# A four-layer model on one core: the second layer's channel mix changes stream, and score products go in pairs of 64-row tiles

## Time and profile before

| what | value |
| --- | --- |
| median of 3 runs | 1272.8 us (1272.34 to 1273.24) |
| the profiled execution, its own time | 1274.41 us |
| its span in the profile | 1272.4 us |
| mean granted TensorE clock | 0.936 of full |
| instructions | 14341 |

### The profile page before, as it was taken

How to read it: one execution, slowest core, us unless ns; L and a number is a source line. 1 busy time by engine, 2 the same in 40 slices (tenths; PEclk the granted TensorE clock), 3 DMA queues, 4 the chain that set the end, 5 groups by cost and what they waited for, 6 DMA issues and landing times.

```text
span 1272.4 us, 14341 instructions
## 1 busy us (share of the span) xinstructions
PE 1124.9 (88%) x5396; PEld 760.6 (60%) x5396; DVE 859.5 (68%) x1152; ACT 501.7 (39%) x1542; POOL 106.6 (8%) x92
## 2 busy tenths in 40 slices
PE   7867889997988999989898879899899998898888
PEld 4634656565755666657565565557656566477665
DVE  4599799688965798799745794466954569444320
ACT  1003125722582257325831624325533255232641
POOL 1020011001100100011000110001020010100000
PEclk8878889998999989989998999998999899899889
DMA  9100000000000000000000000000000000000000
GB/s 368 35 1 0 1 26 5 1 1 25 5 1 1 25 5 2 1 18 13 1 17 9 5 1 1 34 3 10 1 1 33 1 13 1 1 17 1 13 1 17
DMA packets 13895, 22.65 MB, mean 18 GB/s; under 512 B 3841, under 2 KB 10625, under 8 KB 13186
## 3 DMA queue, kind: packets, MB, share of 16 engines
q1 hardware_dynamic: 13826, 21.74, 5.1%
HBM read 16.48 MB, written 2.10 MB: 15 GB/s over the span
## 4 chain that ended last, share of the span: by engine, by line
PE 63%; DVE 24%; ACT 5%; issue 4%; POOL 3%; DMA 1%; SPq 0%; DVEq 0%; POOLq 0%; ACTq 0%
PE PA L1097 7%; PE QA L1003 6%; DVE S_ L509 5%; PE PB L1128 5%; PE QA L1315 5%; PE QB L990 4%; PE QB L1227 3%; PE PA L1036 3%; ACT big L923 3%; DVE az L378 3%; PE QA L1243 3%; DVE A L517 2%; PE QA L990 2%; DVE A L437 2%; PE QA L1306 2%
## 5 line engine op out<-in xcount | busy, mean ns | idle before, releaser
L923 ACT ACTIVATE big<-QB,nmax 128x128 f32<-128x128 f32 x512 | 181.4, 378 | 88.2 <-DVE nmax L632 88.1
L509 DVE TENSOR_TENSOR_SCAN S_<-W_,A 128x1024 f32<-128x1024 f32 x64 | 149.0, 2349 | 0.2
L1128 PE MATMUL PB<-A,common_w 128*128 128x256 f32 x512 | 131.3, 400 | 11.4 <-DVE A L517 11.4
L632 DVE TENSOR_REDUCE nmax<-QB 128x4 f32<-128x512 f32 x128 | 87.1, 685 | 65.6 <-PE QB L1227 41.4
L1128 PEld LDWEIGHTS PB<-A,common_w 128*128 128x128 f32 x512 | 98.3, 201 | 34.6 <-DVE A L517 15.1
L1097 PE MATMUL PA<-rwkv_w,X 128*128 128x256 f32 x384 | 100.8, 416 | 16.8 <-DVE X L416 16.6
L923 ACT ACTIVATION_READ_ACCUMULATOR big<-QB,nmax 128x1 f32 x512 | 111.8, 218 | 0.0
L1227 PE MATMUL QB<-big,QX 128*128 128x256 f32 x384 | 102.8, 392 | 0.0
L1097 PEld LDWEIGHTS PA<-rwkv_w,X 128*128 128x128 f32 x384 | 78.1, 209 | 34.3 <-DVE X L416 21.6
L1243 PE MATMUL QA<-common_w,big 128*128 128x128 f32 x512 | 83.8, 289 | 12.5 <-ACT XT L932 5.9
L1243 PEld LDWEIGHTS QA<-common_w,big 128*128 128x128 f32 x512 | 63.1, 147 | 40.5 <-issue 24.3
(11 more groups left out here) (160 smaller groups left out, 1871.5 us busy)
## 6 DMA issues: line engine op xcount, KB each, us to landing
rwkv_w<-in_rwkv_w SPq DMA_DIRECT2D x2, 2674.0 KB, 14.4
QX<-big SPq DMA_DIRECT2D x96, 32.0 KB, 1.9
attn_w<-in_attn_w SPq DMA_DIRECT2D x2, 1031.5 KB, 16.7
mlp_w<-in_mlp_w SPq DMA_DIRECT2D x1, 2052.0 KB, 23.5
X<-in_x SPq DMA_DIRECT2D x4, 512.0 KB, 13.1
ctx<-in_ctx SPq DMA_DIRECT2D x4, 512.0 KB, 4.2
ctx<-in_ctx_t SPq DMA_DIRECT2D x4, 512.0 KB, 3.5
out<-XT SPq DMA_DIRECT2D x8, 256.0 KB, 2.0
```

The source lines that it names most:

```text
L509: last = v.tensor_tensor_scan(S_[:, d].rearrange("p k t -> p (k t)"), W_[:].rearrange("p k t -> p (k t)"), A_[c % 2][:, d].rearrange("p k ...
L632: v.tensor_reduce(nmax[:, n % 2], bank(2 + n % 2).rearrange("p (j s) -> p j s", j=JH), AX.X, ALU.max, negate=True).then_inc(sem["a_max"], 1)
L923: last = s.activation(PR[:, n % 2, j], bank(2 + n % 2)[:, j * T:(j + 1) * T], ACT.Exp, bias=nmax[:, n % 2, j:j + 1], accum_out=den[:, b, h ...
L1128: last = t.matmul(y, ident, A_[c % 2][:, :, k], start=(c % 2 == 0 and k == 0), stop=False, skip_group_check=True)
```

## The change

It has two parts, with new `ORDER` strings of all engines.

**Channel mix.** It becomes a function of its own on each engine. For the first layer it stays in stream A with the same buffers. For the second layer it is the end of stream R (unit kind `mixer_ffn`): all its products go to PB, its buffers are parts of the recurrence's `A_` and `S_`, it has norm buffers of its own, and since Wk, Wr and Wv share PB, TensorE waits for Relu before `fWr` (g_kr) and for Tanh before `fWv` (g_rr). Three of the last unit's fills (16, 2 and 24 products) go away with it. The next unit's recurrence writes to `A_` after it.

**Scores.** `scores(m)` now issues a pair of jobs: two mask products with 64 rows each, in the tiles at rows 0 and 64, and four float32 products, alternating between the two tiles, one tile's into one bank of QB and the other's into the other bank. For the first sequence the tiles have 32 rows at 0 and 64, or 32 and 96. `QX` has three buffers in which two jobs share 128 rows, so its DMAs wait for no product any more. The pair waits for the exponentials of **both** jobs of the pair ahead. The number of products of each kind stays the same.

```
@@ scores
-                    def scores(n):
-                        b, i = divmod(n, QUAD)
+                    def scores(m):
+                        b, r = divmod(m, 2)
...
-                        if n >= 2:
-                            pe.wait_ge(sem["a_exp"], u.at("a_exp", n - 1))
-                        rows = slice(32 * i, 32 * i + 32)
-                        mask = mrow[:, b * T:(b + 1) * T].unsqueeze(1).broadcast_to([P, JH, T])
-                        t.matmul(bank(2 + n % 2), first_row[:], mask, start=True, stop=False, skip_group_check=True)
-                        if b and i == 0:
-                            pe.wait_ge(q_spread[b % 2], ...)
+                        else:
+                            pe.wait_ge(sem["a_exp"], u.at("a_exp", 2 * m))
+                        for g in range(2):
+                            half = slice(64 * g, 64 * g + 64)
+                            mask = mrow[half, b * T:(b + 1) * T].unsqueeze(1).broadcast_to([64, JH, T])
+                            t.matmul(bank(2 + g), first_row[half], mask, start=True, stop=False,
+                                     tile_position=(64 * g, 0), skip_group_check=True)
+                        if b and r == 0:
+                            pe.wait_ge(q_spread[b - 1], 16 * QUAD * (u.index + 1))
                         for h in range(HALF):
-                            o = bank(2 + n % 2)[:, 2 * h * T:2 * (h + 1) * T]
-                            if b:
-                                last = t.matmul(o, QX[b % 2][:, i, h], K2[:, :, h, b * T:(b + 1) * T], ...)
-                            else:
-                                last = t.matmul(o, Q_[rows, h, 0:T], K2[rows, :, h, 0:T], ..., tile_position=(32 * i, 0))
-                        last.then_inc(sem["a_s"], 1)
+                            for g in range(2):
+                                o = bank(2 + g)[:, 2 * h * T:2 * (h + 1) * T]
+                                if b:
+                                    half = slice(64 * g, 64 * g + 64)
+                                    last = t.matmul(o, QX[b - 1][half, r, h], K2[half, :, h, b * T:(b + 1) * T], ...,
+                                                    tile_position=(64 * g, 0))
+                                else:
+                                    at = 64 * g + 32 * r
+                                    rows = slice(at, at + 32)
+                                    last = t.matmul(o, Q_[rows, h, 0:T], K2[rows, :, h, 0:T], ..., tile_position=(at, 0))
+                                if h == HALF - 1:
+                                    last.then_inc(sem["a_s"], 1)
...
                     scores(0)
-                    yield
-                    scores(1)
                     for n in range(JOBS + 1):
-                        if n + 2 < JOBS:
+                        if n % 2 and n + 1 < JOBS:
                             yield
-                            scores(n + 2)
+                            scores((n + 1) // 2)
@@ DMA queue
-                            if b >= 3:
-                                sp.wait_ge(sem["a_s"], u.at("a_s", QUAD * (b - 2) + i + 1))
-                            sp.dma_start(QX[b % 2][rows, i], Q_[rows, :, b * T:(b + 1) * T]).then_inc(q_spread[b % 2], 16)
+                            sp.dma_start(QX[b - 1][rows, i % 2], Q_[rows, :, b * T:(b + 1) * T]).then_inc(q_spread[b - 1], 16)
@@ TensorE, end of recurrence
+                    if u.kind == "mixer_ffn":
+                        yield from channel_mix(u, "g", in_mixer, False)
@@ TensorE, new function
+                def channel_mix(u, n, w, free):
+                    yield
+                    pe.wait_ge(sem[n + "_z"], u.at(n + "_z", 1))
+                    turn_tokens(lambda h: w["r_out"][:, h * 512:(h + 1) * 512], w["z"], sem[n + "_zT"])
+                    yield
+                    chan_proj(w["k_out"], rh_(u.layer, "fWk"), ..., sem[n + "_k"], ...)
+                    yield
+                    yield from token_proj(w["r_out"], rh_(u.layer, "fWr"), ..., sem[n + "_r"], ...,
+                                          room=lambda k: None if free else pe.wait_ge(sem[n + "_kr"], u.at(n + "_kr", k + 1)))
+                    yield
+                    yield from token_proj(w["v_out"], rh_(u.layer, "fWv"), ..., sem[n + "_v"], ...,
+                                          room=lambda k: None if free else pe.wait_ge(sem[n + "_rr"], u.at(n + "_rr", k + 1)))
@@ buffers
+        in_mixer = dict(CN=split4(A_flat[:, 0:NB * C + HALF * NB]), CS=split4(S_flat[:, 1024:2048]),
+                        C5=[split4(A_flat[:, 2048 + 1024 * i:3072 + 1024 * i]) for i in range(2)],
+                        CK=split4(S_flat[:, 0:1024]), CR=S_flat[:, 1024:2048], cf=S_flat[:, 1024:2048],
+                        z=A_flat[:, 3072:4096]..., bn=gbn, mv=gmv, eps=geps, rstd=grstd)
+        in_mixer.update(k_out=PB, r_out=PB, v_out=PB)
-        QX = [sb(f"QX_{n}", [QUAD, HALF, T]) for n in range(2)]
+        QX = [sb(f"QX_{n}", [2, HALF, T]) for n in range(NB - 1)]
```

More of the change, by code:

```diff
@@ L99 @@
     "VectorE":
[L100 to L104, removed]
@@ L207, in build @@
         RU = sb("RU", [T])
-        A_ = [sb(f"A_{i}", [DC, RS, T]) for i in range(2)]
+        A2 = sb("A2", [2, DC, RS, T])
+        A_ = [A2[:, i] for i in range(2)]
         S_ = sb("S_", [DC, RS, T])
@@ L282, in build @@
                     for n in ("x_done", "ld_x", "ld_small", "ld_mask")}
-        q_spread = [stack.enter_context(nc.semaphore(f"q_spread_{i}")) for i in range(2)]
+        q_spread = [stack.enter_context(nc.semaphore(f"q_spread_{i}")) for i in range(NB - 1)]
         extra = ["ld_ctx", "st_out", "v_chain", "p_chain", "s_chain"]
@@ L579, in attn @@
                             dve.wait_ge(sem["bias_setup"], steps)
[L581 to L605 removed]
+                    if not mlp:
+                        yield from channel_mix(u, "f", in_attn, 0)
                     yield
@@ L833, in recurrence @@
                             .then_inc(sem["r_yn"], 1)
+                    if u.kind == "mixer_ffn":
+                        yield from channel_mix(u, "g", in_mixer)
                 def attn(u):
@@ L844, in norm_x @@
                     def norm_x(k):
+                        if k == 0 and u.stored:
+                            act.wait_ge(sem["st_out"], 32 * u.stored)
                         for h in range(HALF):
@@ L885, in attn @@
                         yield from keys_values()
-                    yield
-                    chan_norm(u, 1, CN, QA, "f_zT", "f_xn")
-                    yield
-                    kf = CK.rearrange("p h b t -> p (h b t)")
-                    for h in range(HALF):
-                        act.wait_ge(sem["f_k"], u.at("f_k", h + 1))
-                        last = s.activation(kf[:, h * 512:(h + 1) * 512], bank(2 + h), ACT.Relu)
-                    link(last)
-                    for h in range(HALF):
-                        s.activation(kf[:, h * 512:(h + 1) * 512], kf[:, h * 512:(h + 1) * 512], ACT.Square).then_inc(sem["f_kk"], 1)
-                    for k in range(2):
-                        yield
-                        act.wait_ge(sem["f_r"], u.at("f_r", k + 1))
-                        s.activation(CR[:, 512 * k:512 * k + 512], bank(k), ACT.Tanh, scale=0.5).then_inc(sem["f_rr"], 1)
+                    if not mlp:
+                        yield from channel_mix(u, "f", in_attn)
                     yield
```

217 lines of the change are left out of this document (125 added, 92 removed).

## The result

The changed kernel takes 1283.9 us (median of 4 runs, 1281.66 to 1287.49); the kernel before took 1272.6 us beside it. The ratio is 1.0091 (95%: 1.0066 to 1.0116): **slower by 0.9%**, where 1231 us were forecast. The profiled execution took 1287.5 us, its span is 1285.5, 13.1 more than before.

A forecast was written before the change was run, and what follows sets the result against it. TensorE was taken to limit seven eighths of the program, then a lone chain at the end. Saved score work -39, pair gaps +15, channel mix -12 and freer order -6 made -42, from 1272.8 to 1231 us; range 1204 to 1268.

The forecast's parts named there:

- seven units of 5.6 us: Units 0 to 6: saving from paired score products on TensorE, together -39 us after counting 0.8 of 49 us.
- its 12, 6 and 15: Last unit's channel mix leaving the lone chain, -12; freer order in units 4 to 6, -6; last unit's pair gaps, +15.
- a cover for the pairs' gap: Units 0 to 6: 20 to 29 steps of other streams, 17 to 30 us, fill the pairs' gap, costing nothing.
- The price of a pair: TensorE's score products: 1.37 us instead of 2.14 for 48 pairs, 1.57 instead of 2.75 for 16; -56 us of work.
- Rivals 2 (in turn): Score pairs: the two tiles share but alternate, so a pair takes six steps; 1242 us, chance 0.13.
- 4 (not together): Score pairs: row tiles do not run together, a pair costs 2.45 us; 1289 us, slower, chance 0.12.
- I count 0.8 of it: First seven units: 0.8 of 49 us saved TensorE work comes off the time, -39 us, VectorE being next in layer one.
- Both banks in step: Last unit's attention: a pair waits for both jobs' exponentials, cycle 5.9 us instead of 3.8; seven gaps, +15 us.
- the upper end of 26: Last unit's pair gaps: +15 us plus 11 more if its jobs ran at 1.2 GHz throughout.
- Part 2: Second layer's channel mix moved to the recurrence's stream: -12 us in the last unit, -6 in units 4 to 6.
- the prediction's own last sentence of "wrong": Sign of failure: last unit's channel mix ends long after unit 6's MLP, leaving it in the lone chain; no size given.
- Rival 3: Attention in all units: pairs' gaps stay unfilled because static orders make TensorE's next step wait; 1278 us, chance 0.13.

The follow-up runs named there:

- the fastest one: Kernel before with the second layer's channel mix moved, single 128-row jobs everywhere, old order strings up to the end of unit 3's attention: 1263.0 us, ratio 0.9917.

## Why the prediction was wrong

With the new strings (TensorE's cut or joined where a pair is) the runs give this account, medians in us:

| step | time | change |
| --- | --- | --- |
| before | 1273 | |
| channel mix moved, new strings, single jobs | 1291 | +18 (spans: first layer +28.0, the rest -11.7) |
| both banks waited for together, two jobs a step | 1303 | +12 |
| tiles side by side | 1284 | -19 |

By stretches, the forecast's seven units of 5.6 us, its 12, 6 and 15 would have been -22 by unit 4, -35 to the end of the last channel mix, +15 behind it. The spans show +19.1, -17.7 and +11.7. Most of the miss, 41 of 55 us, lies in the first layer, for which the forecast named only the saved products.

1. **The new order strings were never priced.** This is the step that failed first; with the third point's it makes the miss, and either of the two put right would by this account have given a faster kernel (some 1256 us without the order's 28, some 1249 with 0.8 of the 68 us counted). The prediction read them once, as a cover for the pairs' gap, and otherwise took the order to be as good as the old one. In the first layer it costs 28 us with the same instructions (665.7 against 637.8). Up to the mark TensorE is idle 106.6 us instead of 88.1, and busy 559.1 instead of 549.7 at a clock of 0.91 instead of 0.93. The waits that grew most between 180 us and unit 4's mark, of the kernel with only the channel mix moved, and of the fastest one:

```profile
PE PB L1179 <- DVE A L561: 16.0, 7, 4.5
PE QB L1260 <- ACT big L957: 12.3, 12, 3.4
PE QA L1282 <- ACT XT L966: 10.6, 4, 4.3
```

```profile
PE PB L1192 <- DVE A L574: 2.8, 2, 2.0
PE QB L1273 <- ACT big L970: 8.5, 11, 2.3
PE QA L1295 <- ACT XT L979: 4.7, 3, 2.5
```

The sums over the state wait 13.2 us more for VectorE's product, the scores 3.8 for exponentials, the turns 5.9 for a copy; other waits shrank, so these three are where the idle time grew and not a sum that makes the 28 us. Which steps stand too early or too late, I haven't taken apart.

2. **The price of a pair was right in kind and too careful in size.** Forecast 1.37 and 1.57 us, measured 1.18 and 1.38: going to 64 rows and back costs 0.10 us (an estimate, 1.18 less five steps of 0.215), not the 0.30 of the earlier trace rows. Saved are 68 us, not 56. The Trainium skill (TensorEngine Tiling, Key Properties) says that a change of mode drains the engine; the trace agrees that there is a price, 0.10 us of the 1.18 that a pair takes. Rivals 2 (in turn) and 4 (not together) are refuted by the same row.

3. **"I count 0.8 of it" is the second step that failed.** Measured is 19 of 68, 0.28. By stretches, in spans between the kernel with the common wait and the changed one: 9.9 us of 34 in the first layer, 8.8 of 25.5 in units 4 to 6; in the last unit, where the saved 8.5 us should have counted in full, the last stretch got no shorter (151.4, then 152.9), its jobs at 0.72 instead of 0.85. A queue that is 89 to 93% busy was taken as a bound from which time can be taken off. Of the 68 us the busy time fell by only 47.5, at the lower clock, and 30.3 us of idle time took most of that back. My reading is that in a static order the streams' waits stand at their own places: where TensorE is early, it waits for VectorE, ScalarE or an in-order copy. No run tests that reading by itself. The 0.8 rested on a busy share and on no row that shows the step behind as ready.

4. **Both banks in step.** Forecast +15 in the last unit, measured +10.1 with pairs (48.1 against 38.0) and +7.6 without (46.0 against 38.4); the upper end of 26, for the low clock, was not reached. In the other units I costed the gap at nothing; the runs say at most some 5 us (3.8, and 1.0 that is within the scatter), so the cover held, nearly.

5. **The channel mix.** Part 2 was put at -12 (23.3 less 11.9 is 11.4) and -6. In the kernels with single jobs its two terms together, with the second layer's new order, gave -11.7: from unit 4's mark to the end of the last channel mix 516.0 us instead of 528.8, and 1 us more behind it. Of these 12.8 us, 8.5 are TensorE's idle time. That -11.7 looks like the -12 alone is luck; no run parts the two terms. In the changed kernel it is hidden by its loss elsewhere: the mix ends no earlier than before (1.4 us later), as the prediction's own last sentence of "wrong" has it, 11.3 us behind unit 6's MLP (1156.6). It is as far behind it in the fastest kernel, where the move pays, so that sign was no sign of a loss.

6. **Rival 3, static orders, at 1278,** came nearest in time, and that is luck in part. Its mark was L923's exponentials well over 25 us; the wait fell to 13.2. But the kind of wait that it named is there at another place: TensorE's step behind a late pair waited 77.7 us for copies instead of 11.1. The common wait accounts for 12 us of the time, and the first layer's order, which the rival did not name, for 28.

## What to carry to other kernels

A kernel whose engines run hand-written or planned orders changes in two parts, the work and the order; price the order by itself, first where the work stays the same, and run the new order with the old work if you can. Do not take an 88% busy engine as a bound: of TensorE work removed, a quarter to a half came off the time here, and of work added 0.7. My explanation, not tested by itself, is that the waits of an in-order program stay where they are. Where a change bundles a gain in one layer with a new order in another, the best version may be half of it: moving the channel mix, with the second layer's new order, and leaving the first layer alone gave 0.9917 (0.9903 to 0.9932).

## What the hardware showed that I had not expected

- **Products of another row tile overtake.** Issued tile by tile, the second tile's mask started 0.23 us after the first tile's, with four float32 records ahead of it in the program. The Trainium skill (TensorE: Matmul & The Clock Gate, Part 3: Packing small matmuls) has products start and end strictly in program order; this trace differs, and the measurement decides. It has a limit: when each tile changes from 64 to 32 rows within its jobs, the second tile waits for the first (2.74 us against 1.38 when both change together).
- **Single jobs in 64-row tiles were granted a lower clock than the same jobs with 128 rows.** In the last unit they had TensorE busy 39.6 of 42.8 us and 52.1 of 54.7, and were granted 0.76 and 0.56; jobs of 128 rows, busy 33.8 of 38.0, were granted 0.87. Why is open: no run tells the rows in use, the tile changes and what came before apart.
- **With products removed, those that stayed were granted a lower clock.** Between the kernel with the common wait and the changed one, which differ in the products side by side, it went from 0.91 to 0.89 in the first layer, from 0.94 to 0.92 in the second and from 0.85 to 0.72 in the last unit's jobs. Of 68 us saved at the full clock, 20 were given back in this way. The order alone took its share before that: 0.96 to 0.93 in the first layer, with no product removed.
